# Splitting weights on VectorE instead of GpSimd, a second memory for half 2's split, and a re-ordered attention section

## The reference

```python
# L0, L2, L3 (L3 with its own gains, same form); role picks one of 3 weight sets per sequence
h = gelu(x @ W_down[role] + b_down[role])
y = x + h @ W_up[role] + b_up[role]
x = layernorm(y) * gamma[role] + beta[role]
# L1
attn = softmax((x @ Wq) @ (x @ Wk).T * scale)          # within one sequence of 32 tokens
attn_out = (attn @ (x @ Wv)) @ Wp + bp
cms_out = gelu(attn_out @ cW1 + cb1) @ cW2 + cb2 + one_hot(target_codes)
modifier = gelu(concat(attn_out, cms_out) @ mW1 + mb1) @ mW2 + mb2
x = clip(x + cms_out + modifier, 0, 1)
```

## Time and profile before

| | us |
|---|---|
| median of 3 runs | 213.95 (213.89, 213.95, 216.11) |
| the profiled execution | 214.72 |
| its span from first to last record | 212.8 |
| PE busy in the span | 186.3 (88%) |
| DVE busy | 121.6 (57%) |
| ACT busy | 82.6 (39%) |
| POOL busy | 69.6 (33%) |

### The profile page before, as it was taken

How to read it: one execution, slowest core, us unless ns; L and a number is a source line. 1 busy time by engine, 2 the same in 40 slices (tenths; PEclk the granted TensorE clock), 3 DMA queues, 4 the chain that set the end, 5 groups by cost and what they waited for, 6 DMA issues and landing times.

```text
span 212.8 us, 3291 instructions
## 1 busy us (share of the span) xinstructions
PE 186.3 (88%) x1101; PEld 161.6 (76%) x1101; DVE 121.6 (57%) x304; ACT 82.6 (39%) x174; POOL 69.6 (33%) x80
## 2 busy tenths in 40 slices
PE   0599988788988699999999999999999999998680
PEld 0487876787966488878888888899999999897360
DVE  5958476596399831999186342033556554556423
ACT  1343563543272930755144442024642444320220
POOL 8377264104518031774063220000214332114211
PEclk9999999999999999999999999999999999999976
DMA  3776379300696202033000000000113522041001
GB/s 87 238 239 201 114 218 226 125 3 2 211 269 214 99 2 99 0 99 102 0 0 0 0 3 0 0 0 8 45 48 113 178 84 79 0 125 47 28 0 51
DMA packets 18587, 17.85 MB, mean 84 GB/s; under 512 B 2049, under 2 KB 16970, under 8 KB 18570
## 3 DMA queue, kind: packets, MB, share of 16 engines
q1 hardware_dynamic: 17288, 15.11, 23.4%
q0 software_dynamic: 1024, 2.37, 4.0%
q10 hardware_dynamic: 258, 0.15, 0.3%
HBM read 16.58 MB, written 1.05 MB: 83 GB/s over the span
## 4 chain that ended last, share of the span: by engine, by line
PE 72%; DVE 13%; issue 4%; ACT 3%; DMA 3%; SPq 3%; DVEq 0%; POOL 0%; ACTq 0%
PE bank L626 17%; PE bank L627 16%; PE bank L628 16%; PE bank L730 6%; PE bank L744 5%; DVE g_l L1357 4%; PE bank L723 3%; DMA wuA<-in_L_cond_W_up 2%; PE bank L688 2%; PE bank L789 2%; DMA role_col_i<-in_itok_B 1%; PE bank L676 1%; PE bank L754 1%; PE bank L725 1%; DVE dots L1325 1%
## 5 line engine op out<-in xcount | busy, mean ns | idle before, releaser
L1357 DVE TENSOR_TENSOR g_l<-g_full,g_h 128x512 fp32r<-128x512 f32 (+1 forms) x40 | 36.6, 925 | 30.6 <-ACT g_h L1000 30.4
L997 ACT ACTIVATE g_full<-bank,vecs 128x512 f32<-128x512 f32 (+1 forms) x40 | 24.2, 604 | 47.9 <-PE bank L628 37.2
L1472 POOL TENSOR_TENSOR rstdA<-rstdA,power 128x1 f32<-128x1 f32 x16 | 9.2, 574 | 53.0 <-DVE rstdA L1217 52.9
L1000 ACT ACTIVATE g_h<-bank,vecs 128x512 fp32r<-128x512 f32 (+1 forms) x40 | 23.9, 598 | 0.0
L1436 POOL TENSOR_TENSOR mw_l<-stage,mw_h 128x1024 fp32r<-128x1024 f32 x6 | 15.3, 2550 | 22.2 <-DVE mw_h L1211 22.2
L626 PE MATMUL bank<-ao_h,mw_h 128*128 128x256 f32 (+1 forms) x48 | 16.7, 348 | 0.0
L1436 POOL TENSOR_TENSOR cw_l<-stage,cw_h 128x1024 fp32r<-128x1024 f32 x4 | 10.8, 2711 | 17.6 <-DVE cw_h L1211 17.6
L626 PE MATMUL bank<-ao_h,cw_h 128*128 128x512 f32 x32 | 13.2, 413 | 3.7 <-ACT g_h L1000 3.7
L626 PE MATMUL bank<-g_h,mw_h 128*128 128x256 f32 (+1 forms) x48 | 16.2, 338 | 0.0
L626 PE MATMUL bank<-cms_h,mw_h 128*128 128x256 f32 (+1 forms) x48 | 15.3, 318 | 0.0
L627 PE MATMUL bank<-cms_l,mw_h 128*128 128x256 f32 (+1 forms) x48 | 15.3, 318 | 0.0
(11 more groups left out here) (232 smaller groups left out, 456.2 us busy)
## 6 DMA issues: line engine op xcount, KB each, us to landing
stage<-in_L_cond_mW SPq DMA_DIRECT2D x6, 512.0 KB, 3.6
wdA<-in_L_cond_W_down SPq DMA_DIRECT2D x20, 128.0 KB, 2.8
wuA<-in_L_cond_W_up SPq DMA_DIRECT2D x20, 128.0 KB, 3.1
stage<-in_L_cond_cW SPq DMA_DIRECT2D x4, 512.0 KB, 3.5
wdB<-in_L_cond_W_down SPq DMA_DIRECT2D x10, 128.0 KB, 2.3
wuB<-in_L_cond_W_up SPq DMA_DIRECT2D x10, 128.0 KB, 3.0
table_gamma<-in_L_cond_ln_w SPq DMA_DIRECT2D x1, 384.0 KB, 6.0
table_beta<-in_L_cond_ln_b SPq DMA_DIRECT2D x1, 384.0 KB, 7.3
```

Of the source, the lines that this page charges most:

```text
L997: act.activation(g_full[n % 2][:, 0:width], bank[b][:, 0:width], ACT.Gelu, bias=bias)
L1000: act.activation(g[0][:, j, 0:width], bank[b][:, 0:width], ACT.Gelu, bias=bias).then_inc(g_high, 1)
L1357: dve.tensor_tensor(g[1][:, j, 0:width], g_full[n % 2][:, 0:width], g[0][:, j, 0:width].bitcast(F32), ALU.subtract).then_inc(g_ready, 1)
L1472: pool.tensor_tensor(var[:, k, 1:2], var[:, k, 0:1], power[:, :], ALU.pow).then_inc(done, 1)
```

## The change

All ten weight pieces are now split on DVE alone; POOL's L1436 is gone. Piece 0 is split in two halves of 512 columns during ticks 3 and 4; pieces 1 and 2 come after `mix(0)`, piece 3 between hidden 1 and hidden 2 of phase 0. Half 2's parts of x get memory of their own (`x1b`, which lies where `g` is written later) and are made in two steps: windows 6 and 7 in tick 7, windows 4 and 5 after both are there. Of the four score blocks DVE copies two and ACT two. Scores of half 1 go to bank 0 rather than bank 2. `project`, `values` and the ticks 7 to 10 are interleaved in a new order. The ten weight passes of L0 use eight slots (four of `wdA`, four of `wdB`), so that only passes 8 and 9 refill one. In the head ACT issues the role column, Wq and Wv, while SP issues the ids, Wk and Wp; DVE's constants that only later work needs stand behind the sort; both folds of Wq and Wk stand ahead of the vectors and of the first `load`. The biases of L2 and L3 (`late_biases`) are made in the head, and the reads of roles by DVE (`value_load`) moved from phase 0 to phase 2.

```diff
-PROJECT_BANKS, SCORE_BANKS = (0, 4), (2, 7)
+PROJECT_BANKS, SCORE_BANKS = (0, 4), (0, 7)
...
+USERS = {"A": [(0, n) for n in (*range(WSLOTS), *range(2 * WSLOTS, PASSES))] + [(2, n) for n in range(PASSES)],
+         "B": [(0, n) for n in range(WSLOTS, 2 * WSLOTS)] + [(3, n) for n in range(PASSES)]}
+
+
+def home(layer, n):
+
+    kind = "A" if (layer, n) in USERS["A"] else "B"
+    return kind, USERS[kind].index((layer, n))
...
-    steps = [("order",), ("chunk_vecs",), ("fold_transpose", 0), ("fold_transpose", 1), ("vectors",), ("fold", 0, 0), ("load", 0, 0),
-             ("fold", 0, 1), ("fold_low", 0)]
+    steps = [("order",), ("fold_transpose", 0), ("fold_transpose", 1), ("spread",), ("fold", 0, 0), ("fold", 0, 1),
+             ("chunk_vecs",), ("vectors",), ("load", 0, 0), ("fold_low", 0)]
...
-    steps.extend([("split", 0)])
+        if t in (3, 4):
+            steps.append(("weights", 0, t - 3))
+    steps.append(("split", 0, 0))
     tick0(7)
-    steps.extend([("project", 0)])
-    tick0(8)
-    steps.extend([("scores", 0)])
-    tick0(9)
-    steps.extend([("probs", 0), ("values", 0)])
-    tick0(10)
-    steps.extend([("split", 1), ("mix", 0), ("project", 1), ("weights", 0), ("values", 1), ("weights", 1),
-                  ("scores", 1), ("probs", 1), ("weights", 2), ("weights", 3)])
-    steps.extend([("hidden", 0, j) for j in range(4)])
+    plain, a, b = ORDER[0][5:]
+    steps.extend([("project", 0, 0), ("turn", 0, plain), ("project", 0, 1), ("split", 1, 0), ("up", 0, b), ("center", 0, a), ("center", 0, b), ("scores", 0), ("turn", 0, a), ("probs", 0), ("turn", 0, b),
+                  ("values", 0, 0), ("values", 0, 1), ("split", 1, 1), ("mix", 0), ("project", 1, 0), ("project", 1, 1),
+                  ("values", 1, 0), ("weights", 1), ("weights", 2), ("scores", 1), ("values", 1, 1), ("probs", 1)])
+    steps.extend([("hidden", 0, 0), ("hidden", 0, 1), ("weights", 3), ("hidden", 0, 2), ("hidden", 0, 3)])
...
-        x1 = [place(f"x1_{x}", [P, KD, HALF], F32R) for x in "hl"]
+        x1 = [[place(f"x1_{x}", [P, KD, HALF], F32R) for x in "hl"],
+              [place(f"x1b_{x}", [P, KD, HALF], F32R, g_at + 4 * JT * HALF + n * 4 * KD * HALF) for n, x in enumerate("hl")]]
...
-            sp.dma_start(role_col_i[:, 0:1], a["itok_B_1_2"].rearrange("(b o) -> b o", o=1)).then_inc(ids_in, 16)
-            sp.dma_start(role_col_i[:, 1:2], a["itok_B_17_1546"].rearrange("(b o) -> b o", o=1)).then_inc(ids_in, 16)
-            for n, pair in enumerate((("L1_cond_Wq", "L1_cond_Wk"), ("L1_cond_Wv", "L1_cond_Wp"))):
-                for m, w in enumerate(pair):
-                    sp.dma_start(tiled(n)[:, KD * m:KD * (m + 1), :],
-                                 a[w].rearrange("(k p) n -> p k n", p=P)).then_inc(stage_in[n], 16)
+            for m, w in enumerate(("L1_cond_Wk", "L1_cond_Wp")):
+                sp.dma_start(tiled(m)[:, KD:2 * KD, :],
+                             a[w].rearrange("(k p) n -> p k n", p=P)).then_inc(stage_in[m], 16)
+            sp.dma_start(role_col_i[:, 1:2], a["itok_B_17_1546"].rearrange("(b o) -> b o", o=1)).then_inc(codes_in, 16)
...
+                kind, i = home(layer, n)
+                slot, down, up, done = (i % WSLOTS, *((wdA, wuA, wA_in) if kind == "A" else (wdB, wuB, wB_in)))
+                if i >= WSLOTS:
+                    user, m = USERS[kind][i - WSLOTS]
+                    if user == 3:
+                        sp.wait_ge(upB_ps, place_of(3, passes_of(3)[m][0]) + 1)
+                    else:
                         sp.wait_ge(upA_ps, lane_a(user, passes_of(user)[m][0]) + 1)
...
+            act.dma_start(role_col_i[:, 0:1], a["itok_B_1_2"].rearrange("(b o) -> b o", o=1)).then_inc(ids_in, 16)
+            for m, w in enumerate(("L1_cond_Wq", "L1_cond_Wv")):
+                act.dma_start(tiled(m)[:, 0:KD, :],
+                              a[w].rearrange("(k p) n -> p k n", p=P)).then_inc(stage_in[m], 16)
...
+                for q in range(2, WB):
+                    lo, hi = S * q, S * (q + 1)
+                    src = bank[SCORE_BANKS[h]][lo:hi, :].rearrange("p (g n) -> p g n", n=P)
+                    ins = act.copy(dots[lo:hi, :, :], src[:, :, lo:hi])
+                ins.then_inc(dots_copied, 1)
...
-            def weights(p):
+            def weights(p, *part):
                 slot, fill = filling(p)
                 _, view, parts = pieces[p]
-                if p == 2:
-                    late_biases()
                 if p == 4:
                     dve.wait_ge(mix_ps, 2 * KD)
                 if p == 8:
                     dve.wait_ge(hidden_ps, 2 * JT)
                 dve.wait_ge(stage_in[slot], 16 * fill + (16 if slot < 2 else 0))
-                dve.tensor_copy(parts[0], view(slot)).then_inc(w_high, 1)
+                high, low, src = parts[0], parts[1], view(slot)
+                if part:
+                    high, low, src = (v[:, part[0] * HID // 2:(part[0] + 1) * HID // 2] for v in (high, low, src))
+                link(dve.tensor_copy(high, src))
+                ins = dve.tensor_tensor(low, src, high.bitcast(F32), ALU.subtract)
+                if part != (0,):
+                    ins.then_inc(w_ready, 1)
...
+            def split(h, part):
+                if h == 0:
+                    dve.wait_ge(x1_window, KD * HALF_FULL)
+                    cols = slice(0, HALF)
+                elif part == 0:
+                    dve.wait_ge(x1_window, KD * FULL)
+                    cols = slice(HALF // 2, HALF)
+                else:
                     dve.wait_ge(x1_rest, len(MESSY))
-                if h:
-                    dve.wait_ge(project_ps, KD * h)
-                    dve.wait_ge(values_ps, 2 * h)
-                src = x1T[:, :, h * HALF:(h + 1) * HALF]
-                link(dve.tensor_copy(x1[0][:, :, :], src))
-                dve.tensor_tensor(x1[1][:, :, :], src, x1[0][:, :, :].bitcast(F32), ALU.subtract).then_inc(x1_split, 1)
+                    cols = slice(0, HALF // 2)
...
-                for q in range(WB):
+                for q in range(2):
...
-            do = {"order": lambda: (find_order(), sort_rest(), first_bias(), sort_codes()), "fold_low": fold, "rest": rest,
+            do = {"order": lambda: (find_order(), sort_rest(), first_bias(), sort_codes(), late_biases()), "fold_low": fold, "rest": rest,
...
-            def weights(p):
-                slot, _ = filling(p)
-                _, view, parts = pieces[p]
-                pool.wait_ge(w_high, p + 1)
-                pool.tensor_tensor(parts[1], view(slot), parts[0].bitcast(F32), ALU.subtract).then_inc(w_ready, 1)
-
```

166 lines of the change are left out of this document (83 added, 83 removed).

## The result

| | before | after |
|---|---|---|
| median, first comparison | 214.47 us (4 runs) | 206.17 us (205.75 to 208.28, 4 runs) |
| the profiled execution | 214.72 | 206.47 |
| its span | 212.8 | 204.6 |
| median, second comparison, another chip | 214.38 (7 runs) | 207.10 (206.67 to 208.24, 4 runs) |

The ratio of after to before is 0.962 (95% interval 0.953 to 0.971), and 0.965 (0.958 to 0.971) in the second comparison. The forecast was 206.8, with a range from 204.2 to 210.0.

What follows compares the result with a forecast made beforehand. It took PE, busy 88% of the span, as the bound, with gaps to win only before 73 us; 6.6 - 0.1 - 0.5 + 1.1 = 7.1 us off 213.95 gave 206.8 us, range 204.2 to 210.0.

Steps and rivals of the forecast that it cites:

- The stretch: Last `down` of layer 0 to first cms_full after `outer(0)`: 50.5 us, 7.5 lost; end at 78.7 instead of 85.29, 6.6 gained.
- Slots: Layer 0's weight passes: eight need no freed slot, so the 1.1 us wait goes and `project(0)` starts without a gap.
- Split: Half 2's x split in two steps, the first ahead of the scores: `project(1)`'s wait of 0.93 us goes.
- Bank and copies: `values(0)` no longer waits 1.2 us for score copies; instead `mix(0)` waits for the probabilities, 1.0 lost.
- Low parts: Weight pieces 0 to 3 on DVE at 2.1 us each: no wait for g_h, which took 3.7 us before.
- Ticks 3 and 4: Layer 0, half of piece 0 in each, about 1.05 us on DVE: 0.1 us lost, at most 2.1.
- Phase 1: Pieces 5, 6 and 7 among eight g_l, 14.5 us on DVE against PE's 11.0: 0.5 us lost, bounds 0 and 2.5.
- Head: Up to the first `down`: earlier sort, row numbers and transposes, full speed possibly earlier; 1.1 us gained, ends 0 and 1.7.
- B: Rival, forecast at a discount: late full speed and more loss in the stretch; 4.0 us gained, 209.9 us; chance 0.2.
- D: Rival, no change: PE's work is untouched and waits move on rather than away; 213.5 us; chance 0.04.
- E: Rival, slower: DVE becomes the bound, each low part taking 2.9 us beside POOL additions; 221.6 us; chance 0.02.
- C: Rival, more than forecast: head gives 1.7 us and the stretch 8; 9.2 gained, 204.7 us; chance 0.12.

Runs made afterwards that it cites:

- c_four_slots: Changed kernel with layer 0's weights back on the four A slots only; 210.84 us, 0.978 of the kernel before.
- i_old_scores: Changed kernel with half 1's scores back in bank 2 and all four copies of each half on DVE; 207.41 us, 0.966 of the kernel before.
- j_pool_late: Changed kernel with low parts on POOL, weight pieces at their old places and `values(1, 1)` ahead of `scores(1)`; 210.94 us, 0.986 of the kernel before.
- a_pool_low: Changed kernel with the low parts of pieces 1 to 9 on POOL again, at the new places; 207.38 us, 0.961 of the kernel before.
- b_dve_low: Kernel before with one edit, all ten low parts on DVE behind their casts; 214.32 us, 0.996 of the kernel before.

## Why the prediction was right, point by point

**The stretch, with the slots and ticks: right in sum, wrong in whom it thanks.** Forecast 6.6 - 0.1 = 6.5, measured 5.75 + 1.13 in front of it, 6.88. By its terms:

- *Slots, 1.1.* The wait is gone after and is back, with 1.4, in c_four_slots. Right. But "`project(0)` starts without a gap" was not: 0.40 go to the wait for x_l.
- *Split, 0.93.* 0.86 by A. Right.
- *Bank and copies, 1.2 replaced by 1.0, so 0.2 net.* Mis-sized: i_old_scores shows 0.77. The wait of `mix(0)` that was to take its place is 0.8, but it is for ACT's copy of the values (values_tok, 43.55 + 0.59 in the chain above), and the kernel before had the same wait in the same place, 0.7; so it was no new one.
- *Low parts.* Here the wrong step is to put the 3.7 us for g_h down to POOL's blocks alone ("POOL's blocks are named for the largest wait"). The blocks were there, but undoing them alone gave 1.32 and left 2.3 us of the wait, and keeping them gave no loss at the new places. The order counted for as much: with pieces 0 to 2 done before the g_l begin, and `values(1, 1)` behind `scores(1)`, A is 1.47 us shorter with DVE and 2.82 with POOL. The two moves were not tested apart. The price of a low part on DVE, 1.23, was right (1.224 to 1.227).
- Of the 6.21 us by which A shrank, 2.81 + 0.86 + 0.77 = 4.44 are shown edit by edit. The other 1.77 were not taken apart by a run. The rows name a candidate for most of them. From the start of `scores(1)` to the first cms_full after `outer(0)` the kernel before takes 30.67 us and j_pool_late 28.97, 1.70 less, and only 0.22 of that is the copies' (i_old_scores against the changed kernel). In that piece the kernel before makes the late biases between the softmax and its casts, 1.13 us of DVE ahead of the first g_l:

```profile
60.97 0.43 DVE L1195 CAST bu_high<-bu_rows 128x512 fp32r<-128x512 f32 x1
61.43 0.75 DVE L1197 SCALAR_TENSOR_TENSOR bu<-bu_high,low_row,bu_rows 128x512 fp32r<-128x512 f32 x1
```

The prediction asked of these two only what they would cost in the head, and not what they gave where they stood. That they are the missing part is likely and not shown.

**Ticks 3 and 4, 0.1 lost: right, at most 0.05 is seen.** From 16.9 us to the last window PE's steps stand where they stood before, to 0.05 us (hA of the last-but-one window at 30.66 and 30.64).

**Phase 1, 0.5 lost; 0.11 measured.** With POOL (a_pool_low) the same piece takes 22.38 instead of 22.51, so DVE's low parts do cost there, a fifth of what I took (before and j_pool_late, both with POOL, take 22.40 and 22.38; b_dve_low, with DVE, 22.52).

**Head, 1.1 gained; 0.16 measured. This is the term that was mis-sized.** Four steps of it failed: "it begins about 0.8 earlier" (the ids land when they did), the row numbers 0.3 earlier (the first gather is 0.69 later), "PE begins the transposes at about 7.2" (8.24), and what stands between folds and `down` in the new order, 1.24 us, was not counted at all. The step "if the change of speed moves forward with the transposes" came out so in this pair, by 1.15 for 1.0, and that was luck: with the transposes at 8.1 to 8.2 us full speed came anywhere from 10.92 to 13.92 in five executions, and in b_dve_low, whose head is that of before, at 13.43 instead of 14.10. The 0.16 is one draw as well: the first `down` starts at 14.2 to 16.8 us in the eight executions with the changed head, and at 15.00 and 15.33 in the two with the old one. The rule of the Trainium skill quoted there ("DMA: Bandwidth & Descriptors", section "Issuing engines are not separate DMA queues"), that a second issuer shares the same engines and saves only the sequencer's time, was the better guide; here not even that time reached the sort.

**What made the total come out.** 6.88 + 0.16 - 0.11 = 6.93 against 7.1 forecast. That it is so near is in part luck: the head gave 0.94 too little, the stretch with the ticks 0.38 and phase 1 0.39 more than forecast. The tail's clock added 1.43 in the profiled pair. The first medians show 8.30 and the second 7.28; the pieces explain 6.93, and how much of the rest is the clock in head and tail the medians can't tell.

**The rivals.** B (209.9) and D (213.5) did not come: no wait took the place of the removed ones in full. E, slower, had its price wrong for this kernel by the rows on mw_l: 1.23 a low part, and not the 2.9 that it took. C's 204.7 would have needed the head; its terms add up to 9.1, not 9.2. Of the signs named, all of "right" came but the last: the first cms_full after `outer(0)` stood at 78.25 and not near 77.7, by the head; of "wrong" one came in part, folds at half speed, up to 13 us.

## What to carry to other kernels

When two engines get in each other's way, ask first whether the colliding work can be done earlier, while nobody waits for either: here the new order gained 1.5 us with one engine and 2.8 with the other (with the move of `values(1, 1)` in it), and changing the engine after it nothing in A. In a sum over a re-ordered head, count what the new order puts last before the next critical instruction, and take the landing time of a small transfer from the trace with its neighbours in flight, not from its issue. Compare by a piece of the trace between two points that the clock and the transfers don't touch: it told 0.1 us where the totals could not tell 2. And read a re-ordered list step by step before naming a run after one of its moves: the kernels that tested the places moved a product too.
